# A prologue in place of two warm-up steps, buffers at multiples of 64 bytes, and values weighed one slot later, in a fused cross-attention and FFN kernel

## The reference, cut to what matters

```python
xn = layernorm(x)
q = xn @ w_q.T + b_q;  k = ctx @ w_k.T + b_k;  v = ctx @ w_v.T + b_v      # 16 heads of 32
attn = softmax(causal(q @ k.T / sqrt(32)))
x = x + tanh(g_xattn) * ((attn @ v) @ w_o.T + b_o)
z = quantise(layernorm(x))            # blocks of 32, scale max|z|/7.5, nearest fp6 value
x = x + tanh(g_ffn) * (z @ quantise(weight).T + bias)
```

## Time and profile before

| what | us |
|---|---|
| median of 3 runs (range) | 1438.02 (1437.79 to 1441.76) |
| the profiled execution, device time | 1438.69 |
| its span, first to last instruction | 1436.9 |
| mean granted TensorE clock | 0.986 of full speed |

### The profile page before, as it was taken

The page is one execution under the profiler, slowest core; times in us unless marked ns, Lnnn a source line. Parts: engine busy times, 40 slices in busy tenths (PEclk is TensorE's granted clock), DMA queues, the critical chain, the costliest instruction groups (busy, mean ns, idle before and its releaser), DMA issues.

```text
span 1436.9 us, 33559 instructions
## 1 busy us (share of the span) xinstructions
PE 1361.0 (95%) x10333; PEld 1190.9 (83%) x10333; DVE 1075.8 (75%) x3802; ACT 984.3 (69%) x3101; POOL 975.6 (68%) x1170
## 2 busy tenths in 40 slices
PE   3789999999999999999999999999999999999976
PEld 3678888888888888888888888888888888888854
DVE  2657777877787787778778777777877787787663
ACT  2567777777767777766767777677777767777651
POOL 2347777767767776776777677777767777776662
PEclk9899999999999999999999999999999999999988
DMA  7645656556555665656565565656556565665420
GB/s 205 168 107 123 157 147 168 152 145 174 133 148 149 161 158 144 170 132 149 148 162 152 145 173 126 152 147 168 151 146 174 128 154 142 167 157 130 112 74 30
DMA packets 169544, 209.32 MB, mean 146 GB/s; under 512 B 19084, under 2 KB 84632, under 8 KB 169368
## 3 DMA queue, kind: packets, MB, share of 16 engines
q1 hardware_dynamic: 167640, 204.03, 55.4%
q10 hardware_dynamic: 1728, 3.15, 0.7%
HBM read 72.88 MB, written 33.55 MB: 74 GB/s over the span
## 4 chain that ended last, share of the span: by engine, by line
PE 82%; SPq 5%; DVE 4%; issue 3%; DMA 3%; ACT 1%; POOL 1%; ACTq 0%; DVEq 0%; POOLq 0%
PE proj L527 20%; PE proj L528 18%; PE proj L529 18%; PE pT_ps L583 10%; PE oT_ps L600 7%; SPq L362 5%; PE s_ps L572 5%; PE s_ps L573 2%; DMA stack<-qk 2%; PE proj L627 2%; DVE qk L912 1%; DMA xs<-in_x 1%; POOL all_probs L444 1%; DVE all_probs L965 1%; ACT qk L734 0%
## 5 line engine op out<-in xcount | busy, mean ns | idle before, releaser
L444 POOL TENSOR_TENSOR all_probs<-all_probs,rden 128x256 f32<-128x256 f32 (+1 forms) x512 | 413.2, 828 | 243.6 <-DVE rden L878 239.6
L705 ACT ACTIVATE all_probs<-all_probs,neg_max 128x128 f32<-128x128 f32 (+1 forms) x1024 | 456.1, 447 | 143.4 <-DVE neg_max L870 136.5
L870 DVE CUSTOM_DVE_ANT_0 all_probs<-s_ps,causal 128x128 f32<-128x128 f32 (+1 forms) x1024 | 321.7, 352 | 154.8 <-PE s_ps L573 154.8
L583 PE MATMUL pT_ps<-ident,all_probs 128*128 128x128 f32 x1536 | 213.0, 275 | 6.0 <-POOL all_probs L444 5.9
L583 PEld LDWEIGHTS pT_ps<-ident,all_probs 128*128 128x128 f32 x1536 | 181.6, 142 | 28.3 <-POOL all_probs L444 7.1
L705 ACT ACTIVATION_READ_ACCUMULATOR all_probs<-all_probs,neg_max 128x1 f32 x1024 | 193.3, 189 | 0.0
L734 ACT ACTIVATE qk<-proj,biases 128x256 fp32r<-128x256 f32 x256 | 105.6, 464 | 103.5 <-DMA stack<-qk 96.8
L965 DVE COPY all_probs<-pT_ps 128x384 f32<-128x384 f32 x256 | 141.5, 553 | 32.9 <-PE pT_ps L583 32.9
L527 PE MATMUL proj<-xT_hi,wq_hi 128*128 128x256 f32 x512 | 157.7, 308 | 5.4 <-DVE wq_lo L833 5.4
L527 PE MATMUL proj<-cT_hi,wk_hi 128*128 128x256 f32 x512 | 152.5, 298 | 6.2 <-POOL cT_lo L460 6.2
L572 PE MATMUL s_ps<-stack 96*128 96x256 f32 x512 | 153.5, 300 | 1.0 <-DVE neg_max L870 1.0
(11 more groups left out here) (105 smaller groups left out, 3645.0 us busy)
## 6 DMA issues: line engine op xcount, KB each, us to landing
stack<-qk SPq DMA_DIRECT2D x768, 128.0 KB, 2.5
c_quads<-in_ctx SPq DMA_DIRECT2D x128, 128.0 KB, 3.0
xs<-in_x SPq DMA_DIRECT2D x32, 512.0 KB, 4.4
xn_rows<-xs SPq DMA_DIRECT2D x32, 512.0 KB, 3.0
x_quads<-xn_rows SPq DMA_DIRECT2D x128, 128.0 KB, 3.1
x<-in_x SPq DMA_DIRECT2D x32, 512.0 KB, 4.8
out<-x SPq DMA_DIRECT2D x32, 512.0 KB, 2.8
all_probs<-in_L_xattn_w_k ACTq DMA_DIRECT2D x4, 256.0 KB, 6.2
```

What stands on the lines that cost most here:

```text
L444: last = nc.gpsimd.tensor_tensor(p, p, wide(rden[:, b % 2, t, h:h + 2], (1 + t) * P), ALU.mult)
L583: last = nc.tensor.transpose(pT_ps[h % 2][:, m * P:(m + 1) * P], probs[:, n % P_RING, m * P:(m + 1) * P], ident[:, :])
L705: last = nc.scalar.activation(probs[:, n % P_RING, cols], probs[:, n % P_RING, cols], ACT.Exp, scale=-1.0, bias=neg_max[:, b % 2, t, h:h + 1],
L870: last = nc.vector.tensor_tensor_reduce(probs[:, n % P_RING, cols], s_ps[h % 2][:, cols], causal[:, (1 - t) * P:], 1.0, MASKED, ALU.add, A ...
```

## The change

1. **A prologue.** The first two steps are replaced by `first()` on each engine. `FIRST` is PE's order: turn k's four chunks, k half 0 of batch 0, turn v, both halves of v, turn q, q half 0, turn o, then `bias_through_o`; then the steps from 2 on. v's rows are now loaded from SP's queue behind x, the small ones and o's follow, then f's (once k is turned), and only then the normalised rows of batch 0 go out, the context of batch 1 comes in, and the quads of x. On DVE the scales of the FFN's weight stand between the turning of x and q's lo parts, and the moments of batch 1 and `bias_v_lo` at the end. In step 2 only f is turned.
2. **The steps.** `AV_SLOTS` goes from (11, 3) to (12, 4), and the weighing now comes right after the slot's scores, ahead of its parts and turnings. `output_hi` follows in the same slot, behind the exponentials and the copy; `output_lo` in the slot after, behind that slot's `maxima`. `OUT_SLOTS` is gone. `SLOT_PARTS` gives slots 3 and 11 four parts (before: one), slots 4 and 12 one (before: two), and others change too; with it o's first part is the first part of slot 5 (before: the third of slot 5). Many stages of `AT` move by a slot or two: context is turned in slots 0 and 1, x in slots 3 and 6. On SP the context quads are issued ahead of the quads of x and of both stacks.
3. **Places.** `biases` has 24 columns, of which 12 are used, and with it the buffers after it start at multiples of 64 bytes. The raw rows of k, q and v change places.

```diff
-AV_SLOTS = (11, 3)
-OUT_SLOTS = (12, 4)
+AV_SLOTS = (12, 4)
-SLOT_PARTS = (2, 4, 2, 1, 2, 4, 2, 4, 2, 4, 2, 1, 2, 4, 2, 4)
+SLOT_PARTS = (2, 4, 2, 4, 1, 3, 2, 4, 2, 3, 2, 4, 1, 4, 2, 2)
...
-    "cT": ((1, 1), (1, 3)), "cT_hi": ((1, 3), (1, 5)), "cT_lo": ((1, 3), (1, 5)),
-    "moments": ((0, 11), (0, 13)), "rstd": ((0, 12), (0, 14)), "xn": ((0, 13), (0, 15)),
-    "xT": ((1, 5), (1, 5)), "xT_hi": ((1, 5), (1, 6)), "xT_lo": ((1, 5), (1, 7)),
...
+    "cT": ((1, 0), (1, 1)), "cT_hi": ((1, 1), (1, 3)), "cT_lo": ((1, 1), (1, 3)),
+    "moments": ((0, 9), (0, 11)), "rstd": ((0, 10), (0, 12)), "xn": ((0, 11), (0, 15)),
+    "xT": ((1, 3), (1, 6)), "xT_hi": ((1, 5), (1, 7)), "xT_lo": ((1, 5), (1, 7)),
...
+FIRST = [*(("w", "k", m) for m in range(4)), ("k", 0, 0), *(("w", "v", m) for m in range(4)), ("v", 0, 0), ("v", 1, 0),
+         *(("w", "q", m) for m in range(4)), ("q", 0, 0), *(("w", "o", m) for m in range(4))]
+FIRST_STEP = 2
+F_TURNS = {(2, 12): (0, 1), (2, 13): (2, 3)}
+BIAS_COLS = 24
...
-        biases = sb("biases", [P, 3 * KC])
+        biases = sb("biases", [P, BIAS_COLS])
...
SP:
+            def first():
+                load_c(0)
+                load_x(0)
+                load_rows("v")
+                load_small()
+                load_rows("o")
+
+                sp.wait_ge(wT_done, whole("k"))
+                load_rows("f")
+                xn_rows(0)
+                load_c(1)
+                xn_quads(0)
+                load_x(1)
...
+                stack_pair(0, 0)
             def step(i):
...
+                if live(i):
+                    load_c(i)
                 if live(i - 1):
...
+                    xn_quads(i - 1)
+                if live(i):
                     load_x(i)
                 if live(i - 2):
                     stack_pair(i - 2, 1)
-                if live(i) and i:
-
-                    sp.wait_ge(turned["cT"], 2 * i)
-                    quads_in(c_quads, ctx_in[i], c_in)
PE:
                     if live(i - 2):
                         scores(i - 2, s)
+                    for b, r in weighed(i, s):
+                        weigh_values(b, r)
                     units(i, s, 0, SLOT_PARTS[s] // 2)
...
                     units(i, s, SLOT_PARTS[s] // 2, SLOT_PARTS[s])
-                    for b, r in weighed(i, s):
-                        weigh_values(b, r)
ACT:
-                    for b, r in put_out(i, s):
-                        output_hi(b, r)
...
                         nc.scalar.activation(probsT[:, h % AV_HEADS + 1, :], pT_ps[1][:, 0:3 * P],
                                              ACT.Copy).then_inc(pT_odd, 1)
+                    for b, r in weighed(i, s):
+                        output_hi(b, r)
DVE:
+            def first():
+                for t in range(T):
+                    turn("cT", 0, t, c_quads, c_in)
+                for t in range(T):
+                    first_moments(0, t)
+                for m in range(KC):
+                    weight_lo(TURNED.index(("k", m)), "k", m)
+                unit("k", 0, 0, bank_of("k", 0, 0))
+                for m in range(KC):
+                    weight_lo(TURNED.index(("v", m)), "v", m)
+                for t in range(T):
+                    turn("xT", 0, t, x_quads, xq_in)
+                weight_scales()
+                for m in range(KC):
+                    weight_lo(TURNED.index(("q", m)), "q", m)
+                unit("q", 0, 0, bank_of("q", 0, 0))
+                for m in range(KC):
+                    weight_lo(TURNED.index(("o", m)), "o", m)
+                for t in range(T):
+                    first_moments(1, t)
+                bias_v_lo()
+                added()
...
                         nc.vector.tensor_copy(probsT[:, h % AV_HEADS, :], pT_ps[0][:, 0:3 * P]).then_inc(pT_even, 1)
+                    for b, r in weighed(i, s - 1):
+                        output_lo(b, r)
                     for unit_ended in ended(i, s):
                         unit(*unit_ended)
...
-                    for b, r in put_out(i, s):
-                        output_lo(b, r)
```

More of the change, by code:

```diff
@@ L92, in live @@
         return 0 <= b < B
-    takers = []
-    for step_no in range(STEPS):
+    takers = [("w", TURNED.index((a, b))) if kind == "w" else (kind, a) for kind, a, b in FIRST]
+    for step_no in range(FIRST_STEP, STEPS):
         for slot_no in range(SLOTS):
@@ L277, in ended, with f_chunks @@
                 lag += slot == 0
[L278 to L287, removed]
+                if at_slot == (slot - 1) % SLOTS and part == PARTS[kind] - 1 and live(i - lag) and (
+                        i - (slot == 0) >= FIRST_STEP):
+                    yield kind, half, i - lag, bank_of(kind, half, i - lag)
+        def f_chunks(i, s):
+            for m in F_TURNS.get((i, s), ()):
+                yield TURNED.index(("f", m)), "f", m
         def columns(kind, t):
@@ L338, in load_small, with xn_rows, xn_quads, load_c @@
                     sp.dma_start(t, across(src)).then_inc(gates_in, 16)
[L340 to L349, removed]
+            def xn_rows(b):
+                sp.wait_ge(xn_ok, 2 * b + 2)
+                sp.dma_start(batch_of(xn_dram, b % 2), xs[:, :, :]).then_inc(xn_out, 16)
+            def xn_quads(b):
+                sp.wait_ge(xn_out, 16 * (b + 1))
+                if b:
+                    sp.wait_ge(turned["xT"], 2 * b)
+                quads_in(x_quads, xn_dram[b % 2], xq_in)
+            def load_c(b):
+                if b:
+                    sp.wait_ge(turned["cT"], 2 * b)
+                quads_in(c_quads, ctx_in[b], c_in)
             def stack_pair(b, half):
@@ L406, in step @@
                     sp.dma_start(batch_of(out, b), x1[:, b % 2, :, :]).then_inc(x1_out[b % 2], 16)
-            for i in range(STEPS):
+            first()
+            for i in range(FIRST_STEP, STEPS):
                 step(i)
@@ L659, in step, with first @@
                     units(i, s, SLOT_PARTS[s] // 2, SLOT_PARTS[s])
-                    for b, r in weighed(i, s):
-                        weigh_values(b, r)
-                    for chunk in chunks_at(i, s):
+                    for chunk in f_chunks(i, s):
                         transpose_weight(*chunk)
-                    if (i, s) == BIAS_AT:
+            def first():
+                for kind, a, b in FIRST:
+                    if kind == "w":
+                        transpose_weight(TURNED.index((a, b)), a, b)
+                    else:
+                        for part in range(PARTS[kind]):
+                            unit(part, kind, a, b)
+                    if (kind, a, b) == ("k", 0, 0):
                         transpose_biases()
-                    if (i, s) == ADD_AT:
-                        bias_through_o()
-            for i in range(STEPS):
+                bias_through_o()
+            first()
+            for i in range(FIRST_STEP, STEPS):
                 step(i)
```

133 lines of the change are left out of this document (68 added, 65 removed), and 4 rows, old and new, of the table WEIGHT_TURNS.

## The result

| | before | after |
|---|---|---|
| median of 4 runs each, us | 1437.9 | 1532.08 |
| lowest to highest, us | 1435.74 to 1441.76 | 1528.5 to 1536.33 |
| profiled execution, us (its span) | 1438.7 (1436.9) | 1532.77 (1530.8) |
| mean granted clock | 0.986 | 0.964 |

The ratio is 1.0653, 95% interval 1.0617 to 1.0689: 94 us more, where 28 were forecast (1466, at most 1503). The direction was right, the size was not.

What follows compares the result with a forecast made beforehand. PE's matmuls and the few waits between them were taken to bound 29 steps of 41.89 us. 1438.7 + 28 (31 steps at +0.90) + 0 (prologue) + 0 (buffers) = 1466.7, given as 1466 us; range 1446 to 1503.

Steps and rivals of the forecast that it cites:

- What goes: Each steady step loses PE's waits at the weighing and in slot 9, 0.76 us, and two groups of parts, 0.1 us.
- What comes, the written order: Slot 5: scores 5, maxima 5, lo, then o make PE wait 1.61 us in each step with an o unit.
- It grows a little by SP's order: x's quads, issued behind the context quads, land later and lengthen the wait at o by 0.15 us, to 1.76.
- The clock rival: Steady steps: the new wait lowers the clock, 1.7 us lost each; half the steps 1492, all 1519 us; chance 0.25.
- Queued behind it: Every later slot runs 1.76 us late, hiding the stacks' 1.4 us delay that would hold up o's second half in slot 9.
- The prologue: Steps 0 to 2: first scores at 57 us, step 2 of 45, step 3 at 102; taken as 0, range -11 to +5.
- Buffers: Buffers at multiples of 64 bytes: k's and q's matmuls gain 0 to 0.5 us a step; taken as 0.

Runs made afterwards that it cites:

- b3: Kernel before with only the weighing of the first half of the heads moved from slot 11 to behind the scores of slot 12: 1421.1 us, ratio 0.9877.
- e1: Kernel after with SP's old step order, x quads first and context quads last: 1467.6 us, ratio 1.0196.
- e2: Kernel after with all of x turned in slot 5, as before: 1462.94 us, ratio 1.0168.
- e10: e1 with the parts of slots 3, 4, 5 and 9 as in the kernel before: 1425.95 us, ratio 0.9914.
- e4: Kernel after with SP's old step order and oT_lo written ahead of the maxima: 1459.72 us, ratio 1.0138.
- e5: Kernel after with the second half of the heads weighed at the end of slot 3 again, hi and lo in slot 4: 1562.11 us, ratio 1.0845.
- e6: e5 with SP's old step order too: 1540.67 us, ratio 1.0685.
- e8: e5 with x turned in slot 5, as before: 1526.83 us, ratio 1.0603.
- e7: Kernel after with a single exchange in SP's step, x quads issued ahead of context quads: 1466.86 us, ratio 1.0182.
- e12: e6 with oT_hi ahead of the exponentials on ACT and oT_lo ahead of the maxima on DVE in slot 4: 1524.39 us, ratio 1.059.
- b2: Kernel before with the wider biases buffer and the new prologue, steps as before: 1427.57 us, ratio 0.9923.
- b1: Kernel before with only the biases buffer widened to 24 columns, so later large buffers start at multiples of 64 bytes: 1433.52 us, ratio 0.9961.
- e3: Kernel after with oT_lo written ahead of the maxima of slots 5 and 13: 1534.32 us, ratio 1.0643.

## Why the prediction had the direction right and the size wrong

**What goes: right, with less in it.** The weighing's waits went, here and in b3, for 18 us or 0.58 a step; the term was 0.76 and 0.1. Slot 9's wait, which was counted in it, did not go: b3 has 3.1 us of it. The rest of the gap stays open; b3 moves only one of the two weighings.

**What comes, the written order: right.** Forecast 1.61 us a step, "whatever the other engines do"; e1 and e2 show 1.54 a step in the view of waits, 28 times each, and e10, which takes most of it away, is 41.7 us faster. The sum with this term and no lateness was 1438.7 + 31 x (1.61 - 0.86) = 1462; e1 took 1467.6, e2 1462.9. That e2 comes so near is in part luck: its steps last 42.96 us instead of 42.64 (9 us over 29 steps), and it reaches step 4 7 us sooner than before (133 against 140.6), where the forecast had no gain. One leg was missed, `oT_hi` and q's lo behind the turning of slot 4, which lies 0.5 us under the one I had (e4: 1.05). It cost the forecast nothing, and my expectations of e4, e5, e6 and e8 a lot.

**"It grows a little by SP's order": this step failed.** It was given 0.15 us a step, and two thirds of the loss hang on it. It put the landing of x's quads at 11.4 us into the step and the harm at 0.15 (0 to 0.4). The landing is at 12.7 on the mean, up to 14.2; DVE stands 3.44 us instead of 2.6, and the wait at o is 2.71 us, 1.17 above e1's. The working had the right chain and no slack in it: from the landing to o it is 4.35 us, so a landing at 11.4 gives o at 15.7 into the step, which is where the written order puts it already (scores 5 some 13.9 us into the step, 0.12 to their second matmul, 1.6 of wait), and by this chain each microsecond later is a microsecond of wait. The issue itself was placed well (6.8, of "7 to 9"). The error is in the 2.6 us from the issue's end to the landing. I took it from the prologue, where these quads were issued with no others just ahead of them; behind the context's quads it is 3.8, and 5.2 in the step above. And 11.4 is the sum with the low end of my own 7 to 9 us; with the high end it is 13.4, which was not carried on. A term at the edge of its cover was given as a point, with a range that came from one row.

**The clock rival: it came true, as the consequence of that step.** I gave it 0.25 for a wait of 1.6 to 1.8 us. That wait never lowered the clock: of 112 waits of 1.0 to 1.6 us in steps 5 to 32 of e1, e2, e4 and e7 none did. Longer waits did at times: in steps 5 to 32 of the kernel after, 16 of the 27 waits over 1.6 us had a fall begin in them or within 2 us behind, the shortest of these 1.85 us, and these are all its falls there (the wait of 3.1 us in step 4 had none); in e6 it was 15 of 34 waits near 2.0 us, in e8 9 of 28. So the late quads cost twice. Of the 58 us between e1 and the kernel after in steps 4 to 32, 34 are PE standing, nearly all of it at o (33 in steps 5 to 32, 75.9 - 43.1), and 24 are PE busy longer, with 58 us at half clock. The rival's "half of the steps" was close (16 of 29), its sum of 1492 was not, since it had only the short wait under it.

**Queued behind it: right, and shown by taking it away.** In the kernel after, PE waits 0.3 us in all for k's lo; in e4, with the wait at o at 1.05 us, 4.2 us, and in e12, without the wait at o, 69.2 us, part of which is e12's own order.

**The prologue: inside its bounds.** First scores at 54.95 us (forecast 57, 55 to 60), step 2 43.7 long (45), step 3 at 98.4 (102, bounds 91 and 107). x's quads landed at 27.84, forecast 29 to 32; in step 2 DVE stood 5.46 us for the next ones, forecast as "some 6 us late". Taken with the old steps it gains 6 us (b2 against b1), where I took 0 with -11 as bound. In the kernel after, step 3, which already has the late quads, gives it back: 45.4 us, 36.8 in b2.

**Buffers: the number inside its bounds, the choice wrong.** I took 0 of 0 to 0.5 us a step; b1 gives 5.7 us, 0.2 a step. The bound was for k's and q's matmuls, but v's, which I had taken as the yardstick since its weight does not move, gained too (rows above): its other operand, `cT`, does move. The median of a stack piece from issue to landing was 2.5 us before and is 2.4 in b1. The estimate from the Trainium skill (DMA: Bandwidth & Descriptors, How a descriptor splits into AXI transactions) was 0.1 us more for the 12 pieces together, 0.01 for one; medians given to 0.1 us show no loss and cannot rule out one so small.

**What stays open.** No run had the long waits without the falls, so the 24 us of longer busy time are put down to the clock by the traces alone. The 9 us of steps 2 and 3 were not taken apart. Why a wait of 2 us is followed by a fall in one step and not in the next is open too. Why v's matmuls are quicker in b1, which operand does it, and whether the 5.7 us are theirs, was not tried.

## What to carry to other kernels

Where two engines follow written orders, add up the order itself first (scores, maxima, lo, o): it gives a floor to the wait that no other view shows. Then look for every transfer whose consumer stands in the same in-order queue ahead of that chain, and price its landing from rows with the same traffic ahead of it, not from a quiet stretch; a landing that ends within a microsecond of its cover is a range, not a term. A wait that is removed uncovers the next (here the stacks), and one of nearly 2 us may cost again by the clock (the shortest with a fall was 1.8 us, in e3).

## What was not expected of the hardware

Only where the buffers start was changed in b1, and the median fell by 0.4%; in the trace, 512-column matmuls of v went from 422 to 416 and from 395 to 390 ns. And the order of two groups of four issues of 128 KB in one queue, 1 MB together, is worth 65 us of 1532, though the DMA engines are busy for only 57% of the time: the group in second place starts 2 us later and lands 0.5 us more slowly.
